# A Householder tridiagonalisation with a second row tile of A x computed as a row on TensorE, its pair slots interleaved, and its zero matmuls dealt out anew

## The reference, cut to what matters

```
deg = A.sum(0) + A.sum(1) - diag(A)
L_norm = d_inv_sqrt[:, None] * (diag(deg) - A) * d_inv_sqrt[None, :]
_, U = eigh(L_norm)
out = U @ (relu(U.T @ h @ W1 + b1) @ W2 + b2)
```

## Time and profile before

| | us |
|---|---|
| median of 3 runs | 4163.15 (4152.97 to 4192.68) |
| span of the profiled execution | 4189.8 |
| PE busy in it | 3382.9 (81%) |
| DVE busy | 3298.6 (79%) |
| ACT busy | 1532.1 (37%) |
| POOL busy | 55.6 (1%) |
| zero matmuls (L206), 2875 records | 845.9 |

### The profile page before, as it was taken

One profiled execution on the slowest core, in us unless ns is written; L12 is line 12 of the kernel. 1 busy time (PEld: TensorE's weight loads), 2 busy tenths in 40 slices (PEclk: granted clock), 3 DMA queues, 4 the chain that ended last, 5 costly groups with the idle time before them and its releaser, 6 DMA issues. The chain is left out here.

```text
span 4189.8 us, 62612 instructions
## 1 busy us (share of the span) xinstructions
PE 3382.9 (81%) x14639; PEld 2049.1 (49%) x14827; DVE 3298.6 (79%) x21659; ACT 1532.1 (37%) x5534; POOL 55.6 (1%) x71
## 2 busy tenths in 40 slices
PE   5999999999999999988886576554207999998859
PEld 3555555555555665577774322243103444454337
DVE  7888898889988788999988899999984323454467
ACT  2444444333333333333332322211212324554545
POOL 0000000000000000000000000000000000020000
PEclk9999999999999899955559887755558999999969
DMA  0000000000000000000000000000002000000001
GB/s 11 1 1 1 1 1 1 1 1 1 1 1 1 1 2 2 1 1 1 1 1 1 1 1 1 1 1 1 0 20 50 0 0 0 1 0 0 0 6 36
DMA packets 14163, 16.47 MB, mean 4 GB/s; under 512 B 571, under 2 KB 10214, under 8 KB 13798
## 3 DMA queue, kind: packets, MB, share of 16 engines
q1 hardware_dynamic: 13798, 12.48, 1.1%
HBM read 8.28 MB, written 4.19 MB: 3 GB/s over the span
## 5 line engine op out<-in xcount | busy, mean ns | idle before, releaser
L206 PE MATMUL ps<-zero_stream 128*128 128x512 bf16 x2875 | 845.9, 397 | 9.0 <-issue 2.8
L206 PEld LDWEIGHTS ps<-zero_stream 128*128 128x128 bf16 x3045 | 333.6, 126 | 227.7 <-issue 101.7
L304 ACT ACTIVATE refl<-ps,tiny 128x1 f32<-128x1 f32 x511 | 133.5, 261 | 451.4 <-PE ps L244 287.9
L318 ACT ACTIVATE vectors<-WihT,refl 128x4 f32<-128x4 f32 (+2 forms) x383 | 115.0, 300 | 391.9 <-DVE refl L439 387.3
L255 PEld LDWEIGHTS ps<-dot_parts,ones 128*128 128x128 f32 x766 | 133.2, 201 | 203.6 <-DVE dot_parts L433 179.9
L233 PE MATMUL ps<-ident,vectors 128*128 128x128 f32 x1148 | 214.9, 298 | 14.3 <-DVE vectors L486 1.3
L380 DVE CUSTOM_DVE_ANT_0 products<-ps,UT 128x511 f32<-128x511 f32 (+60 forms) x426 | 215.0, 533 | 13.1 <-PE ps L233 12.5
L486 DVE SCALAR_TENSOR_TENSOR vectors<-x_scaled,ps,y_scaled 128x4 f32<-128x4 f32 (+3 forms) x510 | 116.2, 228 | 134.5 <-PE ps L255 89.9
L233 PEld LDWEIGHTS ps<-ident,vectors 128*128 128x128 f32 x1148 | 124.0, 141 | 191.6 <-DVE vectors L486 186.0
L380 DVE CUSTOM_DVE_ANT_0 products<-ps,U 128x499 f32<-128x499 f32 (+57 forms) x402 | 199.2, 524 | 5.1 <-PE ps L233 4.6
L686 ACT ACTIVATE sturm_signs<-sturm_products,sign_bias 128x576 bf16<-128x576 f32 x96 | 74.4, 775 | 350.8 <-DVE products_mark L713 350.8
(11 more groups left out here) (611 smaller groups left out, 8440.9 us busy)
## 6 DMA issues: line engine op xcount, KB each, us to landing
out_dram<-x SPq DMA_DIRECT2D x16, 256.0 KB, 2.3
adj<-in_adj_dram SPq DMA_DIRECT2D x1, 1024.0 KB, 5.2
l2w_in<-in_L_gnn_W_dram SPq DMA_DIRECT2D x2, 128.0 KB
Wqkv<-in_L_gnn_Wqkv_dram SPq DMA_DIRECT2D x1, 192.0 KB
L_gnn_W<-in_L_gnn_W_dram SPq DMA_DIRECT2D x2, 64.0 KB
L_gnn_Wg<-in_L_gnn_Wg_dram SPq DMA_DIRECT2D x2, 64.0 KB
x<-in_x_dram SPq DMA_DIRECT2D x4, 0.5 KB
L_gnn_Wo<-in_L_gnn_Wo_dram SPq DMA_DIRECT2D x1, 64.0 KB
```

Source lines behind the costliest of these rows:

```text
L206: nc.tensor.matmul(MA[t][:],still[:,0:P],still[:],start=False,stop=True,skip_group_check=True)
L304: nc.scalar.activation(s[:,u,Y:Y+1],NG[:,0:1] if wide else NG[:,1:2],ACT.Sqrt,bias=tiny[:,0:1]).then_inc(root,1)
```

## The change

In regimes r = 0 to 3 (blocks 1 to 4) it does this:

- A second tile of y goes to PE. The last tile (NT-1) is computed as a row: x broadcast as weights, 128 columns of A moving (`product_as_row`, `y_rows`); ScalarE copies that row to SBUF (`yr`), and PE turns it back to a column (`row_turned`). Tile NT-2 is computed as a column, but in update steps of blocks 1 and 2 it stays with DVE. In the first step of a panel up to m = 129 there is no row, and the last tile is a column. DVE's long products go from three or four to two or three in block 1, and to none in block 3.
- In block 3 the transposes of x go too, and the dots are taken by PE from V and y directly, as in block 4 before; p is made by ScalarE, one activation for each tile.
- The slots of pending pairs are interleaved (u and w side by side). The two correction products become one wide instruction in blocks 1 to 3 (`by_both`), in blocks 1 and 2 the norm is now summed apart from the pairs and ahead of them, as block 3 did. A panel's pairs are first copied by ScalarE (`pairs_turned`), then transposed; two copies of rows follow, not three.
- In blocks 2 and 3 those copies come behind the root on ScalarE. The tile copy comes ahead of p in block 3. x below the diagonal is made by ScalarE (`x_below`), no longer by DVE (L353).
- In block 4 the early selection is two matmuls, and the norm waits for kappa in each step.
- Zero matmuls: `streams` below; in a plain step of blocks 1 and 2 they are one, three and two, in block 3 three, two and two.
- In the last leaf of the eigenvectors two small instructions add a constant.

```diff
+def row_tile(m):
+    if regime(m)==3 or first_of_panel(m) and m<=P+1: return None
+    return NT-1
+def column_tile(m):
+    if row_tile(m) is None: return NT-1
+    return None if update_tile(m) and regime(m)<2 else NT-2
 def pe_tiles(m):
 
-    b=m//P
-    if ends_panel(m) and m<=P or m>PANEL and m%PANEL==1 and b<NT-1: return range(0)
-    return range(NT-1,NT)
+    tiles=[t for t in (column_tile(m),row_tile(m)) if t is not None]
+    return range(min(tiles),NT)
+def rows_of_y(m):
+    return sum(1 for q in range(1,m+1) if row_tile(q) is not None)
 def streams(m):
 
-    b=m//P; kind=2 if ends_panel(m) else 3 if m>PANEL and m%PANEL==1 else 1 if update_tile(m) else 0
-    if b==NT-1: return (0,0,0)
-    return (1 if b<2 else 0,((6,6,9,6),(5,5,4,4),(4,4,3,5))[b][kind],2)
+    kind=3 if first_of_panel(m) else 2 if ends_panel(m) else 1 if update_tile(m) else 0
+    return (((1,3,2),(1,2,2),(1,2,2),(4,2,2)),((1,3,2),(1,2,2),(1,2,2),(3,2,2)),((3,2,2),(2,2,2),(2,2,2),(3,2,2)),((0,0,0),)*4)[regime(m)][kind]
...
+                def row_selected(m, t):
+                    n=2+2*pending(m)[1] if pending(m) else 2
+                    early=m>=TAIL
+                    if early: nc.tensor.matmul(ROWS[:,0:1],pivot(m),XG[:,t,PC_:PC_+1],start=True,stop=True)
+                    lo=2 if early else 0
+                    nc.tensor.matmul(in_pairs(ROWS[:,lo:n]),pivot(m),swapped(XG[:,t,X_+lo:X_+n]),start=True,stop=True).then_inc(sel_ps,1)
...
+                def product_as_row(m):
+                    b=m//P; j=row_tile(m)
+                    if j is None: return
+                    pe.wait_ge(A_copied,copies_of(version(m)))
+                    if m>PANEL: pe.wait_ge(gt_copied,2*((m-1)//PANEL if m<P+PANEL else P//PANEL))
+                    for t in range(b,NT):
+                        ins=nc.tensor.matmul(y_rows(m),XG[:,t,X_:X_+1].broadcast_to([P,P]),A[version(m)%2][:,t,j*P:(j+1)*P],start=t==b,stop=t==NT-1)
...
+                    if regime(m)<2: pe.wait_ge(t2_ready,m)
+                    pe.wait_ge(yr_ready,rows_of_y(m))
...
+                    if r<3:
+                        if r==2: product_as_row(m)
+                        else:
+                            for t in range(b,NT):
+                                ins=nc.tensor.transpose(XR[:,t*P:(t+1)*P],XG[:,t,X_:X_+1].broadcast_to([P,P]),ident[:])
+                            ins.then_inc(xrow_ps,1)
+                        norm(m)
                         if m>1: pe.wait_ge(ub_ready,m-1); pe.wait_ge(w_ready,m-1)
+                        row_selected(m,b)
+                        if r<2: product_as_row(m)
+                        pair_sums(m)
+                        if r==2: product_as_column(m); row_turned(m)
                         streamed(m,streams(m)[0])
+                        if r<2: product_as_column(m); row_turned(m)
+                        if ends_panel(m): transposed(m//PANEL-1)
+                        if update_tile(m): updated(*update_tile(m))
+                        streamed(m,streams(m)[1])
+                        if r<2:
+                            pe.wait_ge(dp_ready,m)
+                            nc.tensor.matmul(dots(m),ones[:],dp[:],start=True,stop=True).then_inc(dot_ps,1)
                         else:
+                            pe.wait_ge(y_ready,m)
+                            for t in range(b,NT):
+                                ins=nc.tensor.matmul(dots(m),V[:,t,m-1:m].broadcast_to([P,P]),XG[:,t,Y_:Y_+2],start=t==b,stop=t==NT-1)
+                            ins.then_inc(dot_ps,1)
...
-                        nc.tensor.matmul(ROWS[:,PC_:last_slot(m+1)],pivot(m+1),XG[:,NT-1,PC_:last_slot(m+1)],start=True,stop=True).then_inc(sel_ps,1)
+                        row_selected(m+1,NT-1)
...
+                    ins=nc.scalar.activation(xm[:,b:b+1],XG[:,b,X_:X_+1],ACT.Copy,scale=below[:,b,i:i+1])
+                    if wide: ins=nc.scalar.copy(xm[:,b+1:NT],XG[:,b+1:NT,X_])
+                    ins.then_inc(xm_ready,1)
+                    if r==0:
                         act.wait_ge(r_ready,m)
+                        nc.scalar.activation(s[:,u,T2:T2+1],norm2(m),ACT.Identity,scale=s[:,u,R:R+1],bias=s[:,u,Y:Y+1]).then_inc(t2_ready,1)
+                    if row_tile(m) is not None:
+                        act.wait_ge(yr_ps,rows_of_y(m))
+                        nc.scalar.copy(yr[:],y_rows(m)[0:1]).then_inc(yr_ready,1)
+                    if r==0:
+                        act.wait_ge(t2_ready,m); act.wait_ge(h_ready,m)
                         nc.scalar.activation(s[:,u,S_:S_+1],s[:,u,T2:T2+1],ACT.Copy,scale=s[:,u,H:H+1]).then_inc(s_ready,1)
+                    if r==2:
+                        act.wait_ge(h_ready,m)
+                        nc.scalar.activation(sh[:,sl],sub[:,sl,i],ACT.Copy,scale=s[:,u,H:H+1]).then_inc(sh_ready,1)
+                    if m>1: reflector_kept(m-1)
+                    if first_of_panel(m) and P<=m<TAIL+PANEL: rows_copied(m//PANEL-1)
                     if update_tile(m): tile_copied(*update_tile(m))
+                    if r>=2:
                         act.wait_ge(y_ready,m)
+                        for t in range(b,NT):
+                            ins=nc.scalar.activation(XG[:,t,PC_:PC_+1],XG[:,t,C_:C_+1],ACT.Identity,scale=s[:,u,S_:S_+1],bias=XG[:,t,Y_:Y_+1])
+                        ins.then_inc(pc_ready,1)
...
+                        pair_parts()
+                        v.wait_ge(A_copied,copies_of(version(m)))
+                        if r<2: v.wait_ge(xrow_ps,m)
+                        if r==0:
+                            multiply(1); inverse(); multiply(1); sign(); multiply(1)
+                            by_both(); corrections(); reflector(); column_of_A(); matrix_times_x(); denominator(); dot_parts(); inverses(); y_below(); p_column()
+                        elif r==1:
+                            multiply(1); inverse(); twice_norm(); multiply(1); sign(); shift(); by_both(); corrections()
+                            reflector(); column_of_A(); matrix_times_x(); denominator(); dot_parts(); inverses(); y_below(); p_column()
                         else:
+                            inverse(); sign(); twice_norm(); by_both(); shift(); corrections(); reflector()
+                            column_of_A(); denominator(); matrix_times_x(); inverses(); y_below()
+                        x_by_shift(); y_scaled(); x_scaled()
...
+                        if j==NL-1 and u==LEAF-1:
+                            for dr in range(2):
+                                v.wait_ge(row,at[dr])
+                                r.inc(nc.vector.tensor_scalar(state[:,dr,0:w],state[:,dr,0:w],PIVOT,None,ALU.add))
```

289 lines of the change are left out of this document (131 added, 158 removed).

## The result

The changed kernel takes 4456.09 us (median of 4 runs, 4405.22 to 4491.21) against 4164.54 (4 runs, 4152.97 to 4192.68): a ratio of 1.066 (95% interval 1.058 to 1.073), slower. It was to be 4156, with a range up to 4235.

A forecast was written before the change was run, and what follows sets the result against it. It took DVE to bound block 1's plain steps, PE its update steps, a latency chain block 4. Blocks 1 to 4 summed as -52 - 4 - 6 + 55 = -7 us, carried to the median 4163.15: 4156, range 4085 to 4235.

The forecast's parts named there:

- PE idles some 0.3 us in a step now: Block 1: PE's gaps no larger than in earlier plain steps, so the 30 us of low clock go.
- PE has no gap in which the clock could fall: Block 3: PE's own work becomes the period, so the 37 us of low clock go.
- rival A: Blocks 1 to 3: the clock keeps falling, the 88 us stay in, +81: 4244, slower; 13%.
- the 88 us of before: Blocks 1 to 3: time lost to low clock before the change, 30, 21 and 37 us, all forecast to go.
- its tile copy ... 0.2 to 0.6 us into the two update steps and the one after them: Block 3: ScalarE's tile copy, now ahead of p, delays three steps of a panel by 0.2 to 0.6 us.
- the new wait for kappa is covered by it: Block 4: the norm's wait for kappa costs nothing beyond the 0.43 us a step of the second selection matmul.
- The 107 ns a load: Block 4: the skill's price for loading 128 columns; by it the extra matmul costs 0.21, the block 27 us.
- the row: Block 4: the trace's low-clock price, 0.42 for a two-instruction pair; by 0.43 a step, 55 us lost.
- DVE idles some 0.5 ahead of the last part of y: Block 1, plain steps: a sign to look for, DVE waiting some 0.5 us until released by PE.
- Rival B: Block 4 pays nothing: PE's fuller queue gets the full clock there, -62: 4101, faster; 15%.
- Rival C: Row's way back longer, blocks 3 and some of 2: copy 0.56, +0.3 in 250 steps, +75: 4231; 12%.
- D: DVE's saving shows: block 1 plain steps fall by 0.45, block 3's ScalarE delays absent, -47: 4116, faster; 8%.

The follow-up runs named there:

- a_rows128: The changed kernel with the panel update contracting over 128 rows instead of 16, the added rows holding zeros: 4215.8 us, ratio 1.010 to the kernel before.
- a_rows128_late: a_rows128 with ScalarE's tile copy of block 3 behind p, b*u and its half, as before the change: 4210 us, one run.
- b_warm6: The kernel before, panel update over 128 rows, zero matmuls per block 4 step: one behind the norm, five behind the product: 4096.1 us, ratio 0.982.

## Why the prediction was wrong, step by step

The step that failed is one sentence in block 1, "PE idles some 0.3 us in a step now, no more than in the plain steps of before (13.71 busy of 14.21), which hold the clock; so the 30 us of low clock go too", and its like in blocks 2 and 3 ("PE has no gap in which the clock could fall"). It took PE's busy time for what keeps the clock. PE did become all but gapless, most of all in block 3 with 697.2 of 698.8 us, and the clock fell as often and stayed down longer. Against a_rows128, whose clock hardly falls, the profiled execution loses 47, 28 and 191 us in blocks 1 to 3, 266 where the blocks grew by 297; by the medians it is 240 (4456 for 4216). The forecast had none of it, and rival A had at most the 88 us of before. That bound was wrong too: a low step's price was taken as given, when moving VectorE's work to PE also made each low step dearer (6.74 for 5.17), and the stretches were three times as long, for which no run gives the cause.

The prices at full clock can be read in a_rows128. Block 1 came to 625.4 for 628, but partly by luck: the plain steps take 4.72 to 4.76 for 4.82, the last two update steps 5.14 and 5.18 for 5.0, and the two misses cancel. Block 2 was 576.1 for 560.5: its steps came 0.1 (plain, 4.35 for 4.25) to 0.2 (second and third, 4.72 and 4.58 for 4.50 and 4.36) dearer, because its path is not PE's chain to the turned row but VectorE's corrections behind the pair sums. Block 3 was 507.9 for 489, plain steps 3.78 for 3.66, the second step 4.06 for 3.85. The term "its tile copy ... 0.2 to 0.6 us into the two update steps and the one after them" held: 0.40 and 0.22 in two of the three by a_rows128_late, 10 us. The update's own 0.3 us for weights over few rows was in no term. Block 4 was right: 452.9 for 447, with the norm at 0.72, and "the new wait for kappa is covered by it" as well, until the cover was taken away. The 107 ns a load of the Trainium skill, *TensorE: Matmul & The Clock Gate*, section "LDWEIGHTS (loading the stationary operand)", gave 27 us, an estimate. The trace does not agree at the low clock: the norm moved by 0.42 for two loads, and the row was right to be preferred.

"DVE idles some 0.5 ahead of the last part of y" was wrong: in a_rows128 it is about 0.1 (L473, 558.72 and 559.01, the first 0.15 long). Its corrections come late themselves, behind the pair sums, which now stand on PE behind the row product.

Rival B asked whether block 4 could get the full clock by a fuller queue. It could not by the change, which added two short instructions; by zero matmuls over all rows it can, and b_warm6 gains 27 us there. Rival C did not come: the copy of the row takes 0.25 us (L357 in m = 102 of a_rows128) for the 0.26 of the forecast. Nor did D: it asked for plain steps of block 1 some 0.45 shorter.

The sum itself has a slip: the 88 us of low clock were read in the profiled execution of before, and the 27 us by which that execution is longer than the median were taken off as well. Executions of the kernel before differ with their clock (4155 us at 0.855, 4191 at 0.84), so part of the gain was counted twice.

With no falls and every price at full clock right, the forecast would have been about 4216 (a_rows128, whose updates are also 0.3 us cheaper). The measured 4456 needed a price for a low step and the length of a stretch, neither of which the earlier trace rows held. The long stretches of before (m = 291 to 296, six steps at the lower level) were the warning that a fall is not over in one step, and I had averaged them into 37 us.

## What to carry to other kernels

A kernel whose clock hangs on filler work has two prices for every edit, one at each level: count what is streamed through the whole array in each step, not PE's busy time, and price the step at the low clock too, since work moved to PE makes each low step dearer. Give matmuls over few rows the full height with rows of zeros where the operands allow it. Run the same code twice before a single block is read: with the clock falling, block 3 took 642 to 699 us here. Where a wait is "covered", write down by what: it comes back when the cover is removed.
